# Where the last batch's output projection stands, and in which order units share a bank, in a transformer kernel on one core

## The chip, the cores and the metric

The kernel runs on one core of one Trainium2 chip. The metric is the device time of one execution in microseconds (us). The engines are called PE (TensorE), ACT (ScalarE), DVE (VectorE), POOL (GpSimd) and SP (SyncE, which here only issues DMAs).

## The reference

```python
x = x + attn(layernorm(x))     # 4 batches, 512 tokens, 256 wide, 16 heads of 16, with softmax
x = x + ffn(layernorm(x))      # silu(x W1^T) * (x W3^T), Walsh-Hadamard, W2^T; 1024 wide
x = x + mem(layernorm(x))      # gated decaying sum along the tokens
x = x + ffn(layernorm(x))
```

Inside `attn`: Q, K, V projections with bias, `scores = Q K^T / 4`, softmax over the keys, the weighted sum of V, and the output projection `out @ Wo.T + bo`. All is float32. The change touches the attention part alone.

## The kernel before

Each float32 product is made of three products of parts: a high part (rounded to the type fp32r) and a low part, what is left (`hi` on ACT, `lo` on POOL or DVE). "Splitting" a tile below means these two operations.

**Steps.** The attention of all four batches is one loop of 128 steps, `K = 32 b + s`: `b` is the batch and `s` (0 to 31) the step in it. A step serves two heads and one tile of 128 keys. In it PE makes two scores with the keys as rows (`score_kq`), ACT takes their exponentials (L921), and at each odd step PE weighs the values of the step pair before the last (`weigh_values`, four matmuls of 32 rows, each in two passes). So that the softmax can't overflow, the maximum of each row of the scores must be known before. For it PE makes each score a second time with the queries as rows, `LEAD = 13` steps ahead (`score_qk`), and DVE takes the maximum of each (`row_max`, L1096). So steps 0 to 18 of the last batch still have maxima beside them, and its steps 19 to 31 have none.

**Groups of maxima.** Eight steps make a group `S`. Once its maxima are there, POOL splits them (`split_max`, `ms<-mxr`, L1362 and L1364), PE turns them (`turn_maxima`, L590), ACT copies them out (`mT`) and SP copies two rows of them into `ring` (`max_copy`), from where the scores of group `S` read them. The turn stands at `s % 8 == MAX_AT` (3), so the last group's stands at step 19 of the last batch, and its rows are first read at step 24.

**Shared bank.** One PSUM bank, `MB`, serves everything else in turn (`shared_bank`): transposes of the normalised x of the next batch (`LN_AT`), its Q and K projections (`QK_AT`), its V projections (`V_AT`) and the output projection of the batch before (`OUT_AT`), of which each half has two parts, one per pair of groups. Each user waits until the one before has been read out; ACT reads out projections and turned maxima, DVE adds the output projection to X (`add_attention`, L1178). In batch 0 the W2 matrix is transformed in these places instead (`HAD_AT`). Each engine runs its own program in order, so a wait holds up everything behind it on that engine. The output projection at batch `b` is that of batch `b - 1`; the one of the last batch itself is made after the loop, in the first MLP chunk.

**Attention output.** Every two groups DVE has a transposed output `AOf`; ACT takes its high part (`AOh`), POOL its low part (`output_lo`, `AOl<-AOf,AOh`, L1342). The first of a batch is split at steps 28 (ACT) and 29 (POOL), the second at steps 5 and 6 of the next batch. `place_values` on POOL adds the bias to V. From step 19 of the last batch DVE and POOL also split the two MLP weights (`ring<-ring`, L1184, L1088, L1342), which the MLP waits for.

**Prologue.** Before step 0 the first batch's maxima of 13 steps are made. POOL there makes the first butterflies of the W2 transform (`fly`, X and PR), takes low parts of q and k (`first_lo`), splits the first maxima, places values; SP and ACT issue DMAs into `ring`.

Of the kernel before, what the change touches and what calls it, by code (L numbers as in the profile page):

```python
# [17 lines left out]
GROUPS = 4  # L18
# [10 lines left out]

LN_AT = (0, 2)  # L30
QK_AT = ((4, 6), (8, 10), (12, 14), (16, 18))
OUT_AT = ((20,), (24, 26))
V_AT = ((22,), (28, 30))

MAX_AT = 3
NORM_AT = (26, 19, 19)
STAT_AT = (18, 12, 12)

# [19 lines left out]
def build(nc, x, wq, wk, wv, wo, bqk_d, bv, bo, mv_, mg, mq, bgq_d, mo, w1, w2, w3, ident_d, had_d, out):  # L58
    ctx = ExitStack()
    with ctx:  # L60
# [197 lines left out]
        def max_copy(S, blk):  # L258
# [2 lines left out]
            r = HALF * blk + MROW  # L261
            return ring[r:r + 2, b % 2, QI, 2 * g:2 * g + 2, :].bitcast(F32), mT[16 * blk:16 * blk + 16, :]

        block = ctx.enter_context(nc.Block())


        @block.sync
        def _(sp):
# [58 lines left out]
                    sp.dma_start(*args).then_inc(ring_in[qk], DMA)  # L327

            ring_load(0, 2)
            ring_load(0, 3)  # L330

            for e in range(2):
# [5 lines left out]
            for b in range(BATCH):  # L338
                for s in range(STEPS):
                    if b == 0 and s == 0:  # L340
                        layout(W_UP, 0, 4, w1)
                        layout(W_LIN, 0, 4, w3)
                    if b == 0 and s == 9:

                        sp.wait_ge(fly_done, 5)
                        for c in range(2, BATCH):
                            sp.dma_start(X[:, c * TT:(c + 1) * TT, :], xv[c, :, :, :]).then_inc(x_in[c], DMA)
                    if b == BATCH - 1 and s == 0:

                        sp.wait_ge(st_ready, 2 * STEPS * b)  # L350
                        weights_in(W_UP)
                        weights_in(W_LIN)
                    if s % 8 == MAX_AT:
                        S = (STEPS * b + s + LEAD) // 8 - 1
                        if S < LAST_GROUP:
                            max_rows(S)
                    if b == 0 and s == 24:

                        for j, src in enumerate((mv_, mg, mq, mo)):
                            layout(W_MEM, j, 1, src)  # L360
                    if b < BATCH - 1:
                        for n in range(4):
                            if s == QK_AT[n][-1] + 2:
                                ring_load(b + 1, n)
# [25 lines left out]
        def _(pe):  # L390
# [189 lines left out]
            def turn_maxima(S, b, s):  # L580

                pe.wait_ge(ml_done, S + 1)
                pe.wait_ge(mt_ready, S)
                if s // 8 == 0:
                    pe.wait_ge(x_f, 2 * (b + 1))
                elif s // 8 < 3 and b < BATCH - 1:
                    pe.wait_ge(qk_f, 4 * b + 2 * (s // 8))
                elif s // 8 == 3:
                    pe.wait_ge(*((x_done, 2 * b) if b else (w2h_done, 3)))
                nc.tensor.transpose(MB[0:32, 0:P], ms[:, :, :, :].rearrange("p a b k -> p (a b k)"), ident[:, :])\  # L590
                    .then_inc(mps_ready, 1)

            def shared_bank(K, b, s):

                more, turned = b < BATCH - 1, (K + LEAD) // 8
                if b and s == LN_AT[0]:

                    pe.wait_ge(xns_ready, b + 1)
                    pe.wait_ge(*((v_copied, 2 * b + 2) if b > 1 else (w2h_done, 4)))
                    ln_transpose(0, MB)  # L600
                if s == LN_AT[b > 0]:
                    pe.wait_ge(x_f, 2 * b + 1)
                    ln_transpose(1, MB)
                for n in range(4):
                    if s in QK_AT[n] and more:
                        if s == QK_AT[n][0]:
                            if n % 2:
                                pe.wait_ge(qk_f, 4 * b + n)
                            else:
                                pe.wait_ge(mt_ready, turned)  # L610
                        i = 3 * QK_AT[n].index(s)
                        project_qk(b + 1, n, range(i, i + 3))
                if b == 0 and s in HAD_AT:

                    j = HAD_AT.index(s)
                    if j == 0:
                        pe.wait_ge(fly_done, 5)
                        pe.wait_ge(mt_ready, turned)
                    elif j == 2:
                        pe.wait_ge(w2h_done, 2)  # L620
                    else:
                        pe.wait_ge(v_copied, 3 + j // 3)
                    mm(MB, had[:, :], fly_half(j // 2)[:, j % 2 * SEQ:(j % 2 + 1) * SEQ], True, True)\
                        .then_inc(had_ready, 1)
                if s == OUT_AT[0][0] and b:
                    pe.wait_ge(aol_done, 2 * b)
                    pe.wait_ge(mt_ready, turned)
                    for part in range(2):
                        out_projection(0, part)
                if s in OUT_AT[1] and b:  # L630
                    if s == OUT_AT[1][0]:
                        pe.wait_ge(*((v_copied, 2 * b + 3) if more else (x_done, 2 * b - 1)))
                    out_projection(1, OUT_AT[1].index(s))
                if s == V_AT[0][0] and more:
                    pe.wait_ge(*((x_done, 2 * b - 1) if b else (w2h_done, 1)))
                    for part in range(2):
                        project_v(b + 1, 0, part)
                if b == 0 and s == V_FIRST_AT[1][0]:
                    pe.wait_ge(mt_ready, turned)
                    for part in range(2):  # L640
                        project_v(1, 1, part)
                if b and s in V_AT[1] and more:
                    if s == V_AT[1][0]:
                        pe.wait_ge(mt_ready, turned)
                    project_v(b + 1, 1, V_AT[1].index(s))

            for K in range(STEPS * BATCH):
                b, s = K // STEPS, K % STEPS
                for h in range(2):
                    wait_kq(K, h)  # L650
                    if K + LEAD < STEPS * BATCH:
                        wait_qk(K + LEAD, h)
                    score_kq(K, h)
                    if K + LEAD < STEPS * BATCH:
                        score_qk(K + LEAD, h)

                shared_bank(K, b, s)
                if K % 2 and K >= 3:
                    weigh_values((K - 3) // 2)
                S = (K + LEAD) // 8 - 1  # L660
                if s % 8 == MAX_AT and S < LAST_GROUP:
                    turn_maxima(S, b, s)

            def ffn_begin():
# [126 lines left out]
        def _(act):  # L791
# [111 lines left out]
            v_evacuate(0, 0, PS[:, V_BANK[0], :])  # L903
            max_evacuate(0, OB)
            act.wait_ge(mt_ready, 1)
            for blk in range(2):
                act.dma_start(*max_copy(0, blk)).then_inc(mrow_in, DMA)  # L907
            v_evacuate(0, 1, PS[:, V_BANK[1], :])
            ln_evacuate(1, 0, MB)
            ln_hi(1, 0, 0)  # L910
# [3 lines left out]
            for K in range(STEPS * BATCH):  # L914
# [29 lines left out]
                    ln_hi(b + 1, 0, 0)  # L944
                if s == LN_AT[b > 0] + 1:
                    ln_hi(b + 1, 1, 0)
                if K == 3:
                    act.wait_ge(wo_in, 8 * DMA)
                    hi(WOh[:, :, :].rearrange("p g n -> p (g n)"), OT[:, :, :].rearrange("p a c -> p (a c)"))\
                        .then_inc(whi_done, 1)  # L950
                if s == 5 and b:
                    act.wait_ge(aof_ready, 2 * b)
                    hi(AOh[:, 3, :], AOf[:, :]).then_inc(aoh_done, 1)
                if s == OUT_AT[1][-1] + 2:
                    act.wait_ge(aof_ready, 2 * b + 1)
                    if b:
                        act.wait_ge(wo_ready, 2 * b)
# [1 line left out]
                if b < BATCH - 1:  # L959
                    for n in range(4):  # L960
                        if s == QK_AT[n][-1] + 1:
                            qk_split(b + 1, n)
                if s % 8 == MAX_AT and (K + LEAD) // 8 - 1 < LAST_GROUP:
                    max_evacuate((K + LEAD) // 8 - 1)
            act.wait_ge(aof_ready, 2 * BATCH)
            hi(AOh[:, 3, :], AOf[:, :]).then_inc(aoh_done, 1)

# [77 lines left out]
        def _(dve):  # L1045
# [143 lines left out]
            for K in range(STEPS * BATCH):  # L1189
                b, s = K // STEPS, K % STEPS  # L1190
                for h in range(2):
                    if K + LEAD < STEPS * BATCH:
                        row_max(K + LEAD, h)
                    if b and h == 0:
                        for half in range(2):
                            if s == OUT_AT[half][-1] + 1:
                                add_attention(b - 1, half)
                S = K // 8 - 1
                if S >= 0:
# [132 lines left out]
        def _(pool):  # L1332
# [105 lines left out]
            for h in range(2):  # L1438

                v, w = (u.rearrange("p (m u n) -> p m u n", u=2, n=D) for u in (fly_raw(h), fly_near(h)))  # L1440
                fly(v[:, :, 0, :], v[:, :, 1, :], w[:, :, 0, :], w[:, :, 1, :])
            first_lo(2)
            first_lo(3)
            split_max(0)
            for h in range(2):

                pool.wait_ge(fly_done, h + 1)
                v, w = fly_near(h), fly_raw(h)
                fly(v[:, 0:SEQ], v[:, SEQ:], w[:, 0:SEQ], w[:, SEQ:])
            pool.wait_ge(const_in, 3 * DMA)  # L1450
            pool.wait_ge(vone_done, 1)
            place_values(0, 0)
            pool.wait_ge(zero_done, 1)
            x_lo_part(1, 0, 0)
            for g in range(1, GROUPS):
                place_values(0, g)

            for K in range(STEPS * BATCH):
                b, s = K // STEPS, K % STEPS
# [7 lines left out]
                    x_lo_part(b + 1, 1, 0)  # L1467
                if s == 6 and b:
                    output_lo(2 * b)
                if s == OUT_AT[1][-1] + 3:  # L1470
                    output_lo(2 * b + 1)
                if b and s in PLACE_MORE:
                    place_values(b, 1 + PLACE_MORE.index(s))
                if b < BATCH - 1:
# [2 lines left out]
                            qk_lo_part(b + 1, n)  # L1477
                    if s == PLACE_AT:
                        place_values(b + 1, 0)
                if K == 5:  # L1480
                    pool.wait_ge(whi_done, 4)
                    lo(WOl[:, :, :].rearrange("p g n -> p (g n)"), OT[:, :, :].rearrange("p a c -> p (a c)"),
                       WOh[:, :, :].rearrange("p g n -> p (g n)")).then_inc(wol_done, 1)
                if K == 4:

                    pool.wait_ge(lnT_ready, 4)
                    pool.wait_ge(x_hi, 4)
# [92 lines left out]
```

## Time and profile before

| | |
|---|---|
| median of 3 runs | 565.23 us |
| the three runs | 564.77, 565.23, 567.7 us |
| the profiled execution's own time | 566.53 us |
| its span | 564.7 us |
| mean granted PE clock | 0.997 |

The profile is of one execution. Its span runs from the first to the last instruction; 1.83 us of its time lie around the span. Times in the trace are us from the span's start. The duration of an instruction contains its latency, so instructions that follow each other closely overlap in it: the distance from start to start is what one costs.

### The profile page before, as it was taken

The numbers are of one execution on the slowest core, as the hardware profiler recorded it, in microseconds if no ns is written. First come the engines' busy times: TensorE is split into PE (matmuls) and PEld (weight loads), VectorE is DVE, ScalarE is ACT, GpSimd is POOL, SyncE is SP. The second block draws the span as 40 slices with busy tenths as digits, with TensorE's granted clock in tenths as the row PEclk, the third lists the DMA queues.
The fourth block names the chain that finished last, engine by engine and source line by source line (L and its number), as shares of the span: only waits on it lengthen the run. The fifth ranks groups of instructions, "written<-read, shape, count | busy, mean of one in ns | idle before, by whom it ended". The sixth has DMA issues, their size and how long they took to land.

```text
span 564.7 us, 8930 instructions
## 1 busy us (share of the span) xinstructions
PE 552.5 (98%) x3220; PEld 383.0 (68%) x3220; DVE 382.9 (68%) x729; ACT 311.8 (55%) x581; POOL 178.4 (32%) x209
## 2 busy tenths in 40 slices
PE   8999999999999998999999999999999999999997
PEld 4543343344434433468888888888888888988887
DVE  6988888898898899836465545746886437363333
ACT  3668889876987797743233223366775333323231
POOL 5794467562546242520202002233332010100100
PEclk9989999999999999999999999999999999999999
DMA  7354540231023030021001020110000210112101
GB/s 231 100 180 146 168 132 3 68 128 34 3 94 133 6 147 3 2 74 25 15 7 31 1 38 2 21 18 1 0 2 1 37 39 15 23 38 38 38 1 37
DMA packets 48443, 29.41 MB, mean 52 GB/s; under 512 B 33496, under 2 KB 41688, under 8 KB 48016
## 3 DMA queue, kind: packets, MB, share of 16 engines
q1 hardware_dynamic: 47180, 27.77, 17.1%
q10 hardware_dynamic: 1220, 1.07, 0.7%
q8 instruction: 26, 0.43, 0.3%
q14 instruction: 17, 0.14, 0.1%
HBM read 10.89 MB, written 5.24 MB: 29 GB/s over the span
## 4 chain that ended last, share of the span: by engine, by line
PE 91%; DVE 4%; ACT 2%; issue 1%; DMA 1%; ACTq 0%; POOL 0%; SPq 0%; POOLq 0%
PE PS L392 89%; DVE mxr L1096 2%; PE PS L403 1%; ACT PR L921 1%; PE PS L590 1%; DMA ring<-mT 1%; DMA X<-in_x 1%; DVE OT L1161 0%; ACTq L883 0%; DVE X L1265 0%; DVE X L1178 0%; ACTq L907 0%; DVE bst L1050 0%; PE PS L527 0%; POOL rstd L1338 0%
## 5 line engine op out<-in xcount | busy, mean ns | idle before, releaser
L392 PE MATMUL PS<-xTh,ring 128*128 128x512 f32 x608 | 188.1, 391 | 0.0
L1096 DVE TENSOR_REDUCE mxr<-PS 128x1 f32<-128x512 f32 x256 | 162.9, 680 | 25.5 <-PE PS L392 24.6
L921 ACT ACTIVATE PR<-PS 128x512 f32<-128x512 f32 x256 | 138.0, 602 | 30.3 <-PE PS L392 29.9
L392 PEld LDWEIGHTS PS<-xTh,ring 128*128 128x128 f32 x608 | 113.2, 188 | 23.7 <-issue 1.7
L392 PE MATMUL PS<-xTl,ring 128*128 128x512 f32 x304 | 110.1, 391 | 0.0
L793 ACT ACTIVATE AOh<-PR 128x512 fp32r<-128x512 f32 x72 | 45.5, 632 | 111.4 <-DVE PR L1235 105.9
L392 PE MATMUL PS<-ring 50*128 50x512 f32 (+1 forms) x512 | 100.0, 454 | 4.4 <-DVE mxr L1096 2.8
L1342 POOL TENSOR_TENSOR xTl<-xf,xTh 128x512 fp32r<-128x512 f32 x30 | 42.4, 1428 | 164.9 <-ACT xTh L793 164.9
L1235 DVE TENSOR_TENSOR PR<-PR,PS 128x512 f32<-128x512 f32 x64 | 43.4, 678 | 71.9 <-PE PS L392 51.8
L392 PEld LDWEIGHTS PS<-ring 50*128 50x128 f32 (+1 forms) x512 | 41.6, 185 | 71.1 <-ACT PR L921 43.2
L1088 DVE TENSOR_TENSOR AOl<-PR,AOh 128x512 fp32r<-128x512 f32 x72 | 51.0, 709 | 45.5 <-ACT AOh L793 45.4
L989 ACT ACTIVATE PR<-PS 128x512 f32<-128x512 f32 x64 | 37.9, 592 | 66.0 <-PE PS L392 65.9
L392 PE MATMUL PS<-W2h,AOh 128*128 128x256 f32 x256 | 72.4, 283 | 0.0
L392 PE MATMUL PS<-W2l,AOh 128*128 128x256 f32 x256 | 72.4, 283 | 0.0
L392 PE MATMUL PS<-W2h,AOl 128*128 128x256 f32 x256 | 72.3, 282 | 0.0
L392 PE MATMUL PS<-PR,Vp 128*32 128x512 f32 x512 | 69.1, 612 | 0.8 <-ACT PR L921 0.8
L392 PEld LDWEIGHTS PS<-xTl,ring 128*128 128x128 f32 x304 | 57.0, 188 | 10.1
L392 PEld LDWEIGHTS PS<-W2h,AOl 128*128 128x128 f32 x256 | 48.9, 191 | 2.1 <-DVE AOl L1088 0.2
L392 PEld LDWEIGHTS PS<-W2l,AOh 128*128 128x128 f32 x256 | 48.9, 191 | 1.9
L392 PEld LDWEIGHTS PS<-W2h,AOh 128*128 128x128 f32 x256 | 48.9, 191 | 0.0
L1335 POOL TENSOR_TENSOR veps<-mom,eps 128x4 f32<-128x4 f32 x16 | 3.2, 200 | 78.3 <-DVE mom L1056 78.3
L392 PEld LDWEIGHTS PS<-PR,Vp 128*32 128x32 f32 x512 | 10.1, 108 | 22.7 <-issue 18.4
(134 smaller groups left out, 623.6 us busy)
## 6 DMA issues: line engine op xcount, KB each, us to landing
ring<-qh SPq DMA_DIRECT2D x48, 128.0 KB, 2.8
xf<-PR SPq DMA_DIRECT2D x112, 32.0 KB, 1.9
ring<-ql SPq DMA_DIRECT2D x24, 128.0 KB, 2.8
ring<-weight_scratch SPq DMA_DIRECT2D x3, 1024.0 KB, 4.8
weight_scratch<-in_w SPq DMA_DIRECT2D x2, 1024.0 KB, 6.8
X<-in_x SPq DMA_DIRECT2D x3, 512.0 KB, 4.7
out<-X SPq DMA_DIRECT2D x6, 256.0 KB, 2.2
X<-in_w SPq DMA_DIRECT2D x1, 1024.0 KB, 5.5
```

Source lines behind the costliest of these rows:

```text
L392: return nc.tensor.matmul(dst, lhsT, rhs, start=start, stop=stop, skip_group_check=True)
L403: last = nc.tensor.transpose(bank[:, t * P:(t + 1) * P], XNs[:, t, dt * P:(dt + 1) * P], ident[:, :])
L590: nc.tensor.transpose(MB[0:32, 0:P], ms[:, :, :, :].rearrange("p a b k -> p (a b k)"), ident[:, :])\
L793: return nc.scalar.activation(dst, src, ACT.Copy, scale=scale)
L921: nc.scalar.activation(PR[:, j % 8, :], PS[:, kq_bank(j), :], ACT.Exp, scale=HD ** -0.5)\
L989: nc.scalar.activation(PR[:, f % 2, :], PS[:, f % 2, :], ACT.Silu).then_inc(sg_done, 1)
L1088: return nc.vector.tensor_tensor(dst, src, h.bitcast(F32), ALU.subtract)
L1096: nc.vector.tensor_reduce(mxr[:, S % 2, blk, TT * p + t:TT * p + t + 1], PS[:, QK0 + i % 3, :], AX.X, ALU.max, negate=True).then_inc(max_d ...
L1235: nc.vector.tensor_tensor(PR[:, 2 + f % 2, :], PR[:, f % 2, :], PS[:, 2 + f % 2, :], ALU.mult)\
L1335: nc.gpsimd.tensor_tensor(veps[:, n0:n0 + count], mom[:, n0:n0 + count, 1], eps[:, n0:n0 + count], ALU.add)\
L1342: return nc.gpsimd.tensor_tensor(dst, src, h.bitcast(F32), ALU.subtract)
```

## The change

The output projection of batch 2, which the last batch carries out at steps 20, 24 and 26, stands at steps 8, 10, 12 and 14 there, where the other batches have Q and K projections. The last turn of maxima stands at step 20 instead of 19, and the last batch's first output is split at steps 21 and 22. In batches 1 and 2 the second half of V (steps 28, 30) and the second half of the output projection (24, 26) change places; the first output of these and of batch 0 is split at step 31 on ACT and at step 2 of the next batch on POOL. In the prologue, POOL runs half of the second butterflies ahead of the split of the first maxima and of the last low part of k; the three later `place_values` go from ahead of the loop to step 4, the butterflies from step 4 to 5; ACT's and POOL's split of Wo go from steps 3 and 5 to 6 and 7; one of the first two row copies goes from ACT's queue to SP's.

```diff
-OUT_AT = ((20,), (24, 26))
-V_AT = ((22,), (28, 30))
-MAX_AT = 3
+OUT_AT = ((20,), (28, 30))
+V_AT = ((22,), (24, 26))
+LAST_OUT_AT = ((8, 10), (12, 14))
+MAX_AT, LAST_MAX_AT = 3, 20
+AO_AT, LAST_AO_AT = STEPS - 1, 21
...
+        def out_at(b):
+            return LAST_OUT_AT if b == BATCH - 1 else OUT_AT
+        def turned_at(K):
+            S = (K + LEAD) // 8 - 1
+            if S == LAST_GROUP - 1:
+                return S if K % STEPS == LAST_MAX_AT else None
+            return S if K % 8 == MAX_AT and S < LAST_GROUP else None
...
             ring_load(0, 2)
+            sp.wait_ge(mt_ready, 1)
+            sp.dma_start(*max_copy(0, 0)).then_inc(mrow_in, DMA)
             ring_load(0, 3)
...
                 if s // 8 == 0:
                     pe.wait_ge(x_f, 2 * (b + 1))
-                elif s // 8 < 3 and b < BATCH - 1:
+                elif b == BATCH - 1:
+                    pe.wait_ge(x_done, 2 * b - 2 + s // 8)
+                elif s // 8 < 3:
                     pe.wait_ge(qk_f, 4 * b + 2 * (s // 8))
-                elif s // 8 == 3:
-                    pe.wait_ge(*((x_done, 2 * b) if b else (w2h_done, 3)))
+                else:
+                    pe.wait_ge(*((v_copied, 2 * b + 4) if b else (w2h_done, 3)))
...
                     pe.wait_ge(xns_ready, b + 1)
-                    pe.wait_ge(*((v_copied, 2 * b + 2) if b > 1 else (w2h_done, 4)))
+                    pe.wait_ge(*((x_done, 2 * b - 2) if b > 1 else (w2h_done, 4)))
                     ln_transpose(0, MB)
...
-                if s == OUT_AT[0][0] and b:
-                    pe.wait_ge(aol_done, 2 * b)
-                    pe.wait_ge(mt_ready, turned)
-                    for part in range(2):
-                        out_projection(0, part)
-                if s in OUT_AT[1] and b:
-                    if s == OUT_AT[1][0]:
-                        pe.wait_ge(*((v_copied, 2 * b + 3) if more else (x_done, 2 * b - 1)))
-                    out_projection(1, OUT_AT[1].index(s))
+                for half in range(2):
+                    at = out_at(b)[half]
+                    if b and s in at:
+                        if s == at[0]:
+                            pe.wait_ge(aol_done, 2 * b)
+                            pe.wait_ge(mt_ready, turned)
+                        for part in range(2) if len(at) == 1 else (at.index(s),):
+                            out_projection(half, part)
...
                     if s == V_AT[1][0]:
-                        pe.wait_ge(mt_ready, turned)
+                        pe.wait_ge(v_copied, 2 * b + 3)
                     project_v(b + 1, 1, V_AT[1].index(s))
...
-            for blk in range(2):
-                act.dma_start(*max_copy(0, blk)).then_inc(mrow_in, DMA)
+            act.dma_start(*max_copy(0, 1)).then_inc(mrow_in, DMA)
...
-                if K == 3:
+                if K == 6:
                     act.wait_ge(wo_in, 8 * DMA)
...
-                if s == OUT_AT[1][-1] + 2:
+                if s == (LAST_AO_AT if b == BATCH - 1 else AO_AT):
                     act.wait_ge(aof_ready, 2 * b + 1)
...
-                            if s == OUT_AT[half][-1] + 1:
+                            if s == out_at(b)[half][-1] + 1:
                                 add_attention(b - 1, half)
...
+            def fly_next(h):
...
-            first_lo(2)
-            first_lo(3)
-            split_max(0)
-            for h in range(2):
...
+            first_lo(2)
+            fly_next(0)
+            split_max(0)
+            first_lo(3)
+            fly_next(1)
...
             x_lo_part(1, 0, 0)
-            for g in range(1, GROUPS):
-                place_values(0, g)
...
-                if s == OUT_AT[1][-1] + 3:
+                if s == 2 and b:
+                    output_lo(2 * b - 1)
+                if s == LAST_AO_AT + 1 and b == BATCH - 1:
                     output_lo(2 * b + 1)
...
-                if K == 5:
+                if K == 7:
                     pool.wait_ge(whi_done, 4)
...
                 if K == 4:
+                    for g in range(1, GROUPS):
+                        place_values(0, g)
+                if K == 5:
```

The loops of SP, PE and ACT ask `turned_at(K)` for the group to turn, where they compared `s % 8` with `MAX_AT` before.

## Rows read from the trace of the kernel before

**Rows 1.** The page's busy times: us, share of the span, instructions.

```profile
PE 552.5 (98%) x3220; PEld 383.0 (68%) x3220; DVE 382.9 (68%) x729; ACT 311.8 (55%) x581; POOL 178.4 (32%) x209
```

**Rows 2.** PE's waits: who waited for whom, us in total, times, longest.

```profile
PE PS L590 <- DVE X L1178: 0.5, 2, 0.3
```

**Rows 3.** PE by stretches: window, us, busy, granted clock, DMA share, GB/s.

```profile
39.20:42.61 3.41, 3.41 (x16) 0.50 0.89 347
...
210.00:222.00 12.00, 10.10 (x69) 1.00 0.01 4
```

**Rows 4.** Timeline of ACT, batch 2: start, us, operation, count, idle before.

```profile
156.72 1.09 ACT L921 ACTIVATE PR<-PS 128x512 f32<-128x512 f32 x2
...
159.94 1.09 ACT L921 ACTIVATE PR<-PS 128x512 f32<-128x512 f32 x2 [0.57 <-PE PS L392]
...
163.38 1.09 ACT L921 ACTIVATE PR<-PS 128x512 f32<-128x512 f32 x2
...
169.84 1.09 ACT L921 ACTIVATE PR<-PS 128x512 f32<-128x512 f32 x2
...
187.66 1.08 ACT L921 ACTIVATE PR<-PS 128x512 f32<-128x512 f32 x2 [0.58 <-PE PS L392]
...
191.43 1.09 ACT L921 ACTIVATE PR<-PS 128x512 f32<-128x512 f32 x2 [0.16 <-PE PS L392]
```

**Rows 5.** Timeline of ACT, batch 3, steps 8 to 31.

```profile
209.88 2.07 ACT L921 ACTIVATE PR<-PS 128x512 f32<-128x512 f32 x4 [0.88 <-PE PS L392]
...
221.60 2.07 ACT L921 ACTIVATE PR<-PS 128x512 f32<-128x512 f32 x4 [0.77 <-PE PS L392]
224.43 2.06 ACT L921 ACTIVATE PR<-PS 128x512 f32<-128x512 f32 x4 [0.77 <-PE PS L392]
...
239.19 0.63 ACT L793 ACTIVATE AOh<-AOf 128x512 fp32r<-128x512 f32 x1
239.71 3.04 ACT L921 ACTIVATE PR<-PS 128x512 f32<-128x512 f32 x6
```

**Rows 6.** Timeline of PE, batch 3, steps 3 to 31.

```profile
203.31 0.28 PE L590 MATMUL PS<-ident,ms 128*32 128x128 f32 x1
...
219.64 0.50 PE L392 MATMUL PS<-ring 50*128 50x512 f32 x2 [0.43 <-DVE mxr L1096]
...
226.77 0.28 PE L590 MATMUL PS<-ident,ms 128*32 128x128 f32 x1 [0.81 <-POOL ms L1364]
...
232.18 0.49 PE L392 MATMUL PS<-ring 50*128 50x512 f32 x2
...
233.51 0.49 PE L392 MATMUL PS<-ring 50*128 50x512 f32 x2
233.94 1.07 PE L392 MATMUL PS<-PR,Vp 128*32 128x512 f32 x8
...
240.85 1.06 PE L392 MATMUL PS<-PR,Vp 128*32 128x512 f32 x8 [0.77 <-ACT PR L921]
```

**Rows 7.** Timeline of POOL, batch 3, steps 1 to 6.

```profile
201.06 1.28 POOL L1342 TENSOR_TENSOR xTl<-xf,xTh 128x512 fp32r<-128x512 f32 x1 [3.14 <-ACT xTh L793]
...
202.67 0.22 POOL L1364 TENSOR_TENSOR ms<-mxr,ms 128x16 fp32r<-128x16 f32 x1
...
206.74 1.28 POOL L1342 TENSOR_TENSOR AOl<-AOf,AOh 128x512 fp32r<-128x512 f32 x1
```

**Rows 8.** Timeline of ACT where batch 0 goes over into batch 1.

```profile
89.23 2.21 ACT L921 ACTIVATE PR<-PS 128x512 f32<-128x512 f32 x4
```

**Rows 9.** Timeline of PE, steps 0 and 3 of batch 0.

```profile
34.58 0.95 PE L392 MATMUL PS<-ring 50*128 50x512 f32 x4 [0.25 <-DMA ring<-mT]
...
39.21 1.93 PE L392 MATMUL PS<-PR,Vp 128*32 128x512 f32 x8
```

**Rows 10.** Timeline of DVE: before step 4 of batch 0, and batch 3 from step 19.

```profile
30.48 9.87 DVE L1096 TENSOR_REDUCE mxr<-PS 128x1 f32<-128x512 f32 x16 [0.16 <-PE PS L392]
...
227.33 0.71 DVE L1172 STREAM_TRANSPOSE AOf<-OTn 128x512 f32<-128x512 f32 x1 [0.96 <-POOL OTn L1381]
...
232.26 1.65 DVE L1088 TENSOR_TENSOR ring<-ring 128x512 fp32r<-128x512 f32 x1
...
237.30 0.99 DVE L1088 TENSOR_TENSOR ring<-ring 128x512 fp32r<-128x512 f32 x1
```

More of the change, by code:

```diff
@@ L352, in _ @@
                         weights_in(W_LIN)
[L353 to L356, printed above, removed]
+                    S = turned_at(STEPS * b + s)
+                    if S is not None:
+                        max_rows(S)
                     if b == 0 and s == 24:
@@ L659, in _ @@
                     weigh_values((K - 3) // 2)
-                S = (K + LEAD) // 8 - 1
-                if s % 8 == MAX_AT and S < LAST_GROUP:
+                S = turned_at(K)
+                if S is not None:
                     turn_maxima(S, b, s)
@@ L962, in _ @@
                             qk_split(b + 1, n)
-                if s % 8 == MAX_AT and (K + LEAD) // 8 - 1 < LAST_GROUP:
-                    max_evacuate((K + LEAD) // 8 - 1)
+                S = turned_at(K)
+                if S is not None:
+                    max_evacuate(S)
             act.wait_ge(aof_ready, 2 * BATCH)
```

## The prediction, before the change was run

> **What bounds the kernel now.** I read the page's busy times first, then the list of waits, then the timelines of ScalarE (ACT), TensorE and GpSimd (POOL) stage by stage. The page is to be read for one thing: TensorE (PE) is busy 98% of the span [rows 1]; its recorded waits are small [rows 2]. So time moves only where PE's own work is moved into a hole, or where PE is made to wait. The edits touch only the attention part, up to about 243 us; behind it PE is busy without such waits, so I count what the attention part gains or loses as the result.
>
> The timeline of ACT gives the length of each step: its two exponentials are issued once a step, so the start of a row is the start of a step. Steps 8 to 15 of batch 2, with the next batch's projections beside the maxima, last from 156.72 to 169.84, 13.12 us [rows 4]. The same steps of batch 3, which have nothing beside the maxima, last from 209.88 to 221.60, 11.72 us [rows 5], and in them PE waits 0.43 us a pair of steps for VectorE's maxima [rows 6]. That is a hole. From step 19 of batch 3 there are no more maxima; there the output projection stands in line with the last scores, and ACT's last exponential ends at 239.71 + 3.04 = 242.75 [rows 5].
>
> **Part 1, the last batch's output projection moved to steps 8 to 14.** One part of it costs PE 232.18 to 233.51 less the score pair in front, which is 233.51 to 233.94: 1.33 - 0.43 = 0.90 us [rows 6]. It is about what three projection matmuls cost a pair of steps in batch 2, so steps 8 to 15 should come to the 13.12 us of [rows 4] with one difference. The half of X that VectorE adds at step 11 must be read out of the shared bank before PE turns the maxima at that same step. That constellation exists before, at steps 26 and 27 of batches 1 and 2: 187.66 to 191.43, 3.77 us, against 159.94 to 163.38, 3.44 us, where the turn waits for no add [rows 4]; the list of waits has PE's two waits for X [rows 2]. So 13.12 + 0.33 = 13.45, and 0.90 instead of 0.89 changes nothing: **+1.75 us**. Low bound 1.4 (no collision at step 11), high bound 4 x 0.90 = 3.6 if the hole took none of it; I take the near end, since batch 2 shows the same work fitted in.
>
> **Part 2, what the tail gives back.** Without the projection the tail is bound by ACT, so I lay out its work. Steps 18 to 31 have 28 exponentials, and six in a row take 3.04, so one costs 0.48 and the last one ends 0.16 after its slot [rows 5]. From 224.43: 28 x 0.48 = 13.44, the split of the attention output 0.52 (239.19 to 239.71) [rows 5], the copy of the turned maxima about 0.25, the tail of the last one 0.16: 238.80. PE can keep up: a pair of steps beside the maxima is four score pairs and a weighing of values, 2.83 us (221.60 to 224.43) [rows 5] less the hole of 0.43; with 1.06 for the weighing [rows 6] a score pair is 0.34, so a pair of steps in the tail, two score pairs and a weighing, is 1.74 us, against 1.92 for four exponentials. What ACT splits at step 21 is VectorE's transpose, done at 227.33 + 0.71 = 228.04 [rows 10]; ACT comes there at about 228.5. The last turn of maxima now comes behind the scores of step 20, so PE's 0.81 us wait for POOL [rows 6] shrinks to about 0.5, and it is no longer on the path that sets the end. The gain is 242.75 - 238.80 = **-4.0 us**. Bounds: -3.4, PE's projection time alone, to -5.0, with PE's waits of 0.81 and 0.77 [rows 6] gone as well.
>
> What is queued behind: the two rows of maxima that SP's queue copies for step 24 are issued some 0.3 us later than before (mT 227.6, not 227.4) but are wanted 1.2 us sooner, at 231.0. VectorE's split of the MLP's weights ended at 237.30 + 0.99 = 238.29 [rows 10]; with two adds fewer and one POOL split (1.28 us) more among them it ends between 237 and 239, and the MLP wants it at 239.9. Both hidden, with about 0.6 and 1 us to spare.
>
> The Trainium skill, "SBUF — State Buffer", section on SBUF's two separate sides, says that VectorE and GpSimd share a port pair that is locked for a whole instruction when VectorE has two SBUF inputs. The trace agrees in kind: a split of these weights took 1.65 us at 232.26 and 0.99 at 237.30 [rows 10]. By that rule the added POOL split can cost the chain all of its 1.28 us; 239.0, still short of 239.9, so the sum stays the same by either.
>
> **Part 3, value and output units change places (batches 1 and 2).** At steps 26 and 27 there is no add before the turn any more, so those pairs go from 3.77 to 3.44 us [rows 4]: **-0.66 us** for two batches. The add moves to step 31, where no turn follows in the same step; the transposes of the next step 0 stand behind two score pairs and a weighing, some 1.6 us later. Bounds: 0, if the wait shows up there instead, to -0.66.
>
> **Part 4, the POOL split that goes from step 29 to step 2.** This is the part that costs. POOL at steps 1 to 3 of a batch: it splits the transposed x, 201.06 to 202.34, then at once makes the high and the low part of the maxima, which end at 202.67 + 0.22 = 202.89. PE turns them at 203.31 [rows 6, 7]. The new split stands between those two in POOL's order, since the one in front waits for ACT's xTh and starts no sooner. It takes 1.28 (the same split at 206.74) [rows 7], so the maxima are ready at 204.17 and PE, which came at 203.31, stands 0.86 us. Behind PE's turn stand the next scores, and for those wait both ACT and VectorE; in batches 1 and 2 PE has no hole later to make it up, in batch 3 VectorE sets the pace and loses the same. In batch 1 there is more: ACT's split of the output moves to step 31, where ACT goes without idle time from step 31 into step 0 (four exponentials in 2.21 against 2.07 elsewhere, a slack of 0.14) [rows 5, 8]; 0.52 - 0.14 = 0.38 us later comes xTh, and with it all of POOL's chain. Batch 1: 1.24, batches 2 and 3: 0.86 each, **+2.96 us**. In batches 2 and 3 ACT has the place, since the value copy left step 30. Bounds: 0, if POOL does the split in its idle time before, to 3 x 1.28 + 0.38 = 4.2.
>
> **Part 5, the prologue.** VectorE's sixteen maxima from 30.48 on run without a gap to 40.35 [rows 10], so they set the pace, and the reordered POOL work (first half of the butterflies, then the maxima's split, then the last split of k) leaves the maxima's split where it was, since it waits for the maxima. One of the two row copies goes by SP's queue instead of ACT's: PE's wait of 0.25 us at 34.58 for them goes [rows 9], **-0.2 us**. The load of the last k rows follows the copy on SP's queue and is issued about 1.4 us later; it is wanted only at step 3. Three placings of values move from ahead of POOL's second split of x to step 4; that split waits for ACT anyway, so the turn at step 3 gains next to nothing. ACT's split of Wo goes from step 3 to step 6 where ACT is nearly full: 0 to 0.5, I take **+0.15**.
>
> The clock stretch deserves its own sentence: at 39.20 to 42.61 the granted clock was 0.50 (the 1.2 GHz level) [rows 3], after steps in which PE had scores alone, with waits between them. The weighing that began at 39.21 took 1.93 [rows 9] instead of 1.06 [rows 6]. I leave this stretch where it is, because the change moves hardly any PE work into the steps before it.
>
> **Sum**: +1.75 - 4.0 - 0.66 + 2.96 - 0.2 + 0.15 = 0.0 us. Made against the profiled execution's own 566.53 us it stays 566.5. That execution is 1.30 above the median of the runs, 565.23, so I predict **565.3 us**.
>
> **Rivals.** *(A) POOL's moved split is hidden.* For it: POOL is idle 3.14 us before 201.06. Against: the order of its program puts the split behind the one that this idle time waits for. Sum without +2.96: 562.3 us; chance 0.14. *(B) The slow clock stretch goes.* The turn and the scores at step 3 and 4 then run at the full level: 1.93 - 1.06 for the weighing and some 0.6 for turn and four scores, -1.5 us, 563.8. For it: PE's work shifts by 0.2 us; against: it shifts nothing else there. Chance 0.18. The Trainium skill, "TensorE: Matmul & The Clock Gate", section on what you observe and what happens, says that the point where the clock changes varies from run to run, which would let (B) come without any cause in the change; the spread of the three runs, 564.77 to 567.7, neither shows nor excludes it. *(C) Slower: the tail falls to the slow clock.* Without the projections PE is busy 1.74 of 1.92 us a pair of steps. If the clock drops there for 3.41 us as at 39.20, PE does 1.7 us of work where 3.1 are due: +1.4, 566.7. It decides where PE's idle share is much above that of the maxima stage of batch 3, whose holes (0.43 of 2.83) left the clock at 1.00 [rows 3]. Chance 0.08. *(D) The maxima's rows for step 24 land late*, over 231.0 less 0.5: each us more is a us lost; if they take 3.0 us from the issue of the second copy at 228.3, +0.8, 566.1. Chance 0.10.
>
> **How the numbers follow.** Forecast 0.42, (A) 0.14, (B) 0.18, (C) 0.08, (D) 0.10, none of these 0.08. About 0.5%, 2.8 us, is what a measurement of this kernel tells from no change: under 562.4 is faster, over 568.1 slower. (A) falls on that edge, and with (B) beyond it; none of the rivals alone reaches 568.1. Faster 0.16, same 0.77, slower 0.07. The range 562.2 to 567.4 just holds (A), and the prices of (B), (C) and (D) and the bounds of part 5; it leaves out the unnamed cases and (A) with more besides.
>
> **What would show it.** Steps 8 to 15 of batch 3 at about 13.45 us; from the last step with maxima to the last exponential 14.4 instead of 18.3; PE waiting for POOL's low part of the maxima near step 3 of batches 1 to 3, about 1.2, 0.9 and 0.9 us; step pairs 26 and 27 at 3.44. I am wrong if there is no such wait, if the tail stays at 18, or if the granted clock differs from before in a stretch.

## The result, and the profile after

The changed kernel takes 570.95 us (median of 5 runs, 569.79 to 581.22) beside 565.23 us (median of 5 runs, 564.77 to 567.7): the ratio is 1.0093, with a 95% interval of 1.0072 to 1.0113. It is slower by 0.9%, clear of the 0.5% that I had named, and outside the range I gave (562.2 to 567.4).

The first profile of it was taken in an execution of 581.22 us, in which the granted clock was at its lower level for two long stretches, 20.5 us from 38.7 and 10.2 us from 246.9. A second profile of the same kernel (own time 569.88 us, span 568.1, mean granted clock 0.996) is nearer to the median, and the rows below are of that one. The page's busy times:

```profile
PE 553.6 (97%) x3220; PEld 383.1 (67%) x3220; DVE 385.9 (68%) x729; ACT 311.9 (55%) x581; POOL 178.4 (31%) x209
```

PE has lost one per cent of its busy share. Its waits (waited for, us in total, times, longest us):

```profile
PE PS L407 <- DVE OT L1177: 3.7, 1, 3.7
PE PS L607 <- POOL ms L1380: 2.6, 4, 1.0
```

The first wait did not exist before: one wait of 3.7 us for VectorE's transpose into `OT`. The second is the one I had forecast, POOL's low part of the maxima, at step 3 of batches 1 to 3; its fourth time, at step 20 of batch 3, stands for the single 0.8 us at step 19 before.

The timeline of ACT, with the starts of steps 26 and 28 of batch 2, and of steps 8 and 16 of batch 3 and its end:

```profile
188.38 1.09 ACT L936 ACTIVATE PR<-PS 128x512 f32<-128x512 f32 x2 [0.58 <-PE PS L407]
...
191.84 1.09 ACT L936 ACTIVATE PR<-PS 128x512 f32<-128x512 f32 x2 [0.16 <-PE PS L407]
...
211.04 1.09 ACT L936 ACTIVATE PR<-PS 128x512 f32<-128x512 f32 x2 [0.86 <-PE PS L407]
...
224.43 2.11 ACT L936 ACTIVATE PR<-PS 128x512 f32<-128x512 f32 x4 [0.57 <-PE PS L407]
227.40 3.08 ACT L936 ACTIVATE PR<-PS 128x512 f32<-128x512 f32 x6 [0.86 <-PE PS L407]
...
231.47 0.62 ACT L809 ACTIVATE AOh<-AOf 128x512 fp32r<-128x512 f32 x1
232.00 5.97 ACT L936 ACTIVATE PR<-PS 128x512 f32<-128x512 f32 x12
242.08 4.27 ACT L936 ACTIVATE PR<-PS 128x512 f32<-128x512 f32 x8 [4.12 <-PE PS L407]
```

Against [rows 4]: the pair of steps 26 and 27 takes 3.46 us instead of 3.77. Against [rows 5]: steps 8 to 15 take 13.39 instead of 11.72, and step 18 to the last exponential 242.08 + 4.27 - 227.40 = 18.95 instead of 18.33. The tail goes at ACT's full pace for twelve exponentials, as I had laid it out, and then ACT stands idle for 4.12 us. PE in the same stretch:

```profile
235.09 0.73 PE L407 MATMUL PS<-ring 50*128 50x512 f32 x4
239.54 1.78 PE L407 MATMUL PS<-PR,Vp 128*32 128x512 f32 x8 [3.72 <-DVE OT L1177]
241.25 1.22 PE L407 MATMUL PS<-ring 50*128 50x512 f32 x4
242.40 1.42 PE L407 MATMUL PS<-PR,Vp 128*32 128x512 f32 x8
```

The weighing at 239.54 is the first of the last group. It writes the bank that VectorE's transpose of the group before must have read (`pe.wait_ge(ot_done, S)` in `weigh_values`). VectorE meanwhile:

```profile
230.93 4.02 DVE L1200 CAST ring<-ring 128x512 fp32r<-128x512 f32 x4
234.99 1.65 DVE L1104 TENSOR_TENSOR ring<-ring 128x512 fp32r<-128x512 f32 x1
236.56 1.48 DVE L1200 CAST ring<-ring 128x512 fp32r<-128x512 f32 x1
238.08 0.69 DVE L1104 TENSOR_TENSOR ring<-ring 128x512 fp32r<-128x512 f32 x1
238.69 0.71 DVE L1177 STREAM_TRANSPOSE OT<-PS 128x512 f32<-128x512 f32 x1
```

It works through the MLP's weights without idle time and comes to the transpose at 238.69. PE had finished what the transpose reads at about 235.1. So the transpose was held up by what stands ahead of it in VectorE's program. In the kernel before the same two instructions, the transpose and PE's weighing behind it, were:

```profile
235.07 0.72 DVE L1161 STREAM_TRANSPOSE OT<-PS 128x512 f32<-128x512 f32 x1
...
236.69 1.06 PE L392 MATMUL PS<-PR,Vp 128*32 128x512 f32 x8
```

There the transpose ended at 235.79, 0.9 us before PE came. Counted from the start of step 18 (224.43 before, 227.40 now), PE comes 3.8 us sooner than before, and the transpose ends 0.6 us later.

Behind the wait the granted clock is at 0.50 (PE: window, us, busy, clock, DMA share, GB/s), and the last weighings cost 1.4 to 1.8 us instead of 1.06:

```profile
210.00:224.40 14.40, 14.12 (x101) 1.00 0.01 3
...
239.80:243.20 3.40, 3.40 (x16) 0.50 0.02 5
```

POOL at the head of batch 3 answers to [rows 7]:

```profile
201.46 1.28 POOL L1358 TENSOR_TENSOR xTl<-xf,xTh 128x512 fp32r<-128x512 f32 x1 [9.05 <-ACT xTh L809]
202.69 1.28 POOL L1358 TENSOR_TENSOR AOl<-AOf,AOh 128x512 fp32r<-128x512 f32 x1
203.91 0.20 POOL L1378 CAST ms<-mxr 128x16 fp32r<-128x16 f32 x1
204.19 0.22 POOL L1380 TENSOR_TENSOR ms<-mxr,ms 128x16 fp32r<-128x16 f32 x1
```

and PE turns the maxima only then:

```profile
202.74 1.06 PE L407 MATMUL PS<-PR,Vp 128*32 128x512 f32 x8
204.47 0.28 PE L607 MATMUL PS<-ident,ms 128*32 128x128 f32 x1 [0.66 <-POOL ms L1380]
```

### The profile page after: what moved, and what is told of

Its sections match the earlier page's. It is cut to its first block, busy times and chain, and to the rows that moved or that the text cites. A ratio compares the mean times of both kernels' runs of the same rounds, so it can differ in the third digit from the quotient of the medians.

```text
span 579.4 us, 8933 instructions
## 1 busy us (share of the span) xinstructions
PE 563.5 (97%) x3220; PEld 385.7 (67%) x3220; DVE 385.1 (66%) x729; ACT 312.4 (54%) x581; POOL 177.7 (31%) x209
## 3 DMA queue, kind: packets, MB, share of 16 engines
q10 hardware_dynamic: 1202, 1.06, 0.6%
## 4 chain that ended last, share of the span: by engine, by line
PE 80%; DVE 7%; issue 6%; POOL 5%; DMA 1%; ACT 1%; ACTq 0%; SPq 0%; POOLq 0%
PE PS L407 79%; DVE mxr L1112 3%; DVE ring L1200 1%; POOL XNs L1361 1%; POOL Vp L1387 1%; PE PS L418 1%; DVE OT L1177 1%; DMA X<-in_x 1%; POOL xTl L1358 1%; POOL AOl L1358 1%; POOL W2l L1358 0%; PE PS L607 0%; DVE bst L1066 0%; POOL OTn L1397 0%; POOL rstd L1354 0%
## 5 line engine op out<-in xcount | busy, mean ns | idle before, releaser
L407 PE MATMUL PS<-ring 48*128 48x512 f32 (+1 forms) x512 | 104.0, 471 | 2.2 <-DVE mxr L1112 0.8
L407 PEld LDWEIGHTS PS<-ring 48*128 48x128 f32 (+1 forms) x512 | 42.8, 193 | 73.5 <-ACT PR L936 38.5
L407 PE MATMUL PS<-PR,Vp 128*32 128x512 f32 x512 | 73.9, 651 | 3.9 <-DVE OT L1177 3.7
L407 PEld LDWEIGHTS PS<-xTl,ring 128*128 128x128 f32 x304 | 57.1, 188 | 10.2
```

The costliest lines, as they stand in the source:

```text
L407: return nc.tensor.matmul(dst, lhsT, rhs, start=start, stop=stop, skip_group_check=True)
```

## The experiments

Theory V: the loss is the wait for VectorE's transpose, which stands behind splits of the MLP's weights. Rival C: the granted clock falls in the tail or the prologue by itself, and the wait is a small part. Beside them stand POOL's moved split and the prologue as smaller terms. Except for the two single runs, ratios are to the kernel before, run beside the others on the same chip; its medians in the three sets of runs were 565.39 us (the first four experiments), 566.2 (the next four) and 565.67 (the last two).

**The change again.** No edit.

> The changed kernel itself, for a second profile, since in the first one the granted clock was at its lower level for 20.5 us from 38.7 and for 10.2 us from 246.9. Theory V (VectorE's order in the tail): PE still waits 3.5 to 3.9 us for VectorE's transpose of the output near step 27 of batch 3, because that transpose stands behind six splits of MLP weights; the clock stretch behind it is a consequence and may be shorter. Theory C (the clock is the cause by itself): with a shorter stretch at the lower level the wait shrinks too, to under 2 us. Both: steps 3 of batches 1 to 3 at about 2.5 us, as in the first profile.

Measured: one run of 569.88 us; the wait is 3.72 us as in the first profile (3.74), and steps 3 take 2.60, 2.49 and 2.50 us. The lower clock lasted 3.4 us in the tail here and 10.2 there, and the wait did not change with it: against C. Here it began at 239.8, when the wait was over.

**VectorE's splits of the second weight behind the transpose.**

```diff
+SPLIT_STEPS = (19, 20, 21, 22, 26, 27, 28, 29)
-                if b == BATCH - 1 and SPLIT_AT <= s < SPLIT_AT + 8:
-                    w_split_hi((s - SPLIT_AT) // 4, (s - SPLIT_AT) % 4)
+                if b == BATCH - 1 and s in SPLIT_STEPS:
+                    i = SPLIT_STEPS.index(s)
+                    w_split_hi(i // 4, i % 4)
```

> The changed kernel with one edit: VectorE splits the second MLP weight at steps 26 to 29 of batch 3, behind the transpose of step 25, and not at 23 to 26. Theory V: the 3.7 us wait goes, the stretch from step 18 to the last exponential falls from about 19 to 20 us to 14.4 to 15, and the time falls by 4 to 6 us, to 565 to 567. Theory C: the clock falls there anyway, the time stays at 570 to 571. Rival L (the MLP then waits for the late splits): the wait moves behind the last step, 1 to 2 us, time 566 to 569.

Measured: 566.46 us, ratio to the kernel before 1.0022 (0.9996 to 1.0048): 4.5 us less than the changed kernel. The wait of 3.7 us is gone, and the tail runs through at ACT's pace. ACT:

```profile
235.47 3.08 ACT L937 ACTIVATE PR<-PS 128x512 f32<-128x512 f32 x6 [0.86 <-PE PS L408]
238.44 0.26 ACT L810 ACTIVATE mT<-PS 32x128 f32<-32x128 f32 x1
238.60 1.06 ACT L937 ACTIVATE PR<-PS 128x512 f32<-128x512 f32 x2
239.55 0.62 ACT L810 ACTIVATE AOh<-AOf 128x512 fp32r<-128x512 f32 x1
240.07 9.88 ACT L937 ACTIVATE PR<-PS 128x512 f32<-128x512 f32 x20
```

From 235.47 to 249.95 are 14.48 us; my sum had 14.37. In the whole tail the clock stayed at its full level in this profile. The MLP did not wait for the later splits (rival L falls): from the last exponential to the end of the span are 321.8 us, 321.7 in the changed kernel.

**POOL's split at step 0.**

```diff
-                if s == 2 and b:
+                if s == 0 and b:
                     output_lo(2 * b - 1)
```

> The changed kernel with one edit: POOL makes the low part of the last output at step 0 of the next batch, ahead of its idle time, and not at step 2. If the 0.7 to 0.8 us by which step 3 of batches 1 to 3 grew come from this split in front of the maxima's, steps 3 go back from 2.5 to about 1.8 us and the time falls by 2.2 us, to 568.7. If they come from the later split on ACT (step 31) alone, nothing falls: 570.9.

Measured: 570.82 us, ratio 1.0084 (1.0053 to 1.0115). The median hardly moved, but the trace shows the term: steps 3 of batches 1 to 3 take 1.63, 1.76 and 1.76 us instead of 2.60, 2.49 and 2.50, in all 2.44 less. The wait of 3.7 us is still there, and in five of the seven runs the mean granted clock was 0.988 or less, in only one of the five runs of the changed kernel. In runs with the same mean clock, 0.994, this kernel took 568.15 and 568.59 us and the changed one 570.71, 570.95 and 571.63: 2.6 us apart in the middle, near the 2.44 of the trace. Why so many of its runs had a lower clock stays open.

**Both.** The two edits above together.

> The changed kernel with both edits of the two kernels before. Theory V with the POOL term: the gains add, 4 to 6 and 2.2 us, time 562.5 to 565, under the kernel before. Theory C: 568.7.

Measured: 563.87 us, ratio 0.9955 (0.9928 to 0.9982), below the kernel before. The longest wait of PE in the tail is 0.3 us.

**The last batch's edits alone.** The kernel before with the edits that concern batch 3: `out_at`, `turned_at`, and

```diff
-                if s == OUT_AT[1][-1] + 2:
+                if s == (LAST_AO_AT if b == BATCH - 1 else OUT_AT[1][-1] + 2):
...
-                if s == OUT_AT[1][-1] + 3:
+                if s == (LAST_AO_AT + 1 if b == BATCH - 1 else OUT_AT[1][-1] + 3):
                     output_lo(2 * b + 1)
```

> The kernel before with the last batch's edits alone: its output projection at steps 8 to 14, the last turn of maxima at step 20, the last output split at steps 21 and 22. Theory V: all of the tail's loss is in this part. Steps 8 to 15 take 13.5 us instead of 11.7, PE waits 3.5 to 3.9 us for VectorE's transpose, and the tail (step 18 to the last exponential) takes 18 to 20 us instead of 18.3: in all +1.8 to +3.5 us, 567.2 to 569 beside 565.4. If the tail needs the other edits to go wrong, it takes 14.4 us and the time is 563.2.

Measured: 571.43 us, ratio 1.0079 (1.0053 to 1.0104). Its waits:

```profile
PE PS L403 <- DVE OT L1176: 3.7, 1, 3.7
```

Steps 8 to 15 take 13.49 us and the tail 18.92. So the loss of the tail needs nothing else of the change. The median lies above what I expected; its two runs of mean clock 0.994 took 568.19 and 568.74 us, in the expected span, and the rest had lower clocks. In its profile the lower clock also stood for 17.1 us from 22.9 and for 6.8 us from 46.8, far ahead of the wait, and that part of the time is not explained by the tail.

**The last batch's edits with the late splits.** The kernel of before with these edits and `SPLIT_STEPS`.

> The kernel before with the last batch's edits and VectorE's splits of the second MLP weight behind the transpose of step 25. Theory V: tail 14.4 to 14.5 us, steps 8 to 15 13.5, time -2.1 us against the kernel before, 563.3. It has neither the swap of steps 24 to 30 (-0.65) nor the two extra splits; the two kernels should lie under 0.5 us apart.

Measured: 562.88 us, ratio 0.9947 (0.9924 to 0.997). Steps 8 to 15 take 13.49 us, the tail 14.49. So the idea of the change was worth about 2 us in the kernel before, once the one thing behind which it waited was out of the way: the trace gives 1.77 + 0.12 - 3.84 = -1.95 us (steps 8 to 15, steps 16 and 17, the tail), and among runs with a mean clock of 0.999 or 1.000 the medians are 562.85 and 565.04, 2.2 apart. The ratio shows more, 3.0 us, because 16 of the 24 runs of the kernel before had a lower clock and only 2 of these 10.

**Both, with the prologue as before.** The changed kernel with the two edits of "Both", called mends from here on, and all prologue edits taken back (POOL's order, the row copy on ACT's queue, placings, ACT's split of Wo at step 3 and POOL's at step 5).

> The kernel with both mends (weight splits late, POOL's split at step 0) and with all prologue edits taken back. If the prologue edits cost (ACT's split of Wo at step 6: steps 4 to 31 of batch 0 took 48.6 to 48.75 us instead of 48.13), those steps fall back to 48.1 and the time falls by 0.3 to 0.5 us, to 563.4. If they gain as I took it, it rises by 0.2.

Measured: 563.1 us, ratio 0.9931 (0.9894 to 0.9968). Steps 4 to 31 of batch 0 take 48.27 us instead of 48.63: the prologue edits cost 0.4 us there. One profile of each carries this; the two times, 563.1 and 563.87, point the same way and do not settle it.

**The last output split late.** The change with `LAST_AO_AT = 28`.

> The changed kernel, but with the last batch's first output split at steps 28 (ACT) and 29 (POOL), not 21 and 22. It tells apart the order on VectorE and the port that VectorE shares with GpSimd. If the order of the program decides, PE still waits at least 2.4 us for the transpose, by no more than 1.3 us less than 3.7. If the added POOL split holds VectorE up, the wait falls under 2 us.

Measured: one run of 570.92 us. The wait is 2.73 us. VectorE:

```profile
231.69 4.04 DVE L1200 CAST ring<-ring 128x512 fp32r<-128x512 f32 x4
235.76 1.65 DVE L1104 TENSOR_TENSOR ring<-ring 128x512 fp32r<-128x512 f32 x1
237.33 0.41 DVE L1200 CAST ring<-ring 128x512 fp32r<-128x512 f32 x1
237.78 0.69 DVE L1104 TENSOR_TENSOR ring<-ring 128x512 fp32r<-128x512 f32 x1
238.39 0.71 DVE L1177 STREAM_TRANSPOSE OT<-PS 128x512 f32<-128x512 f32 x1
```

POOL beside it, in the changed kernel and here:

```profile
236.05 1.71 POOL L1358 TENSOR_TENSOR ring<-ring 128x512 fp32r<-128x512 f32 x1
...
232.62 4.24 POOL L1358 TENSOR_TENSOR ring<-ring 128x512 fp32r<-128x512 f32 x3 [0.36 <-DVE ring L1200]
```

POOL's last split of the weights ended at 237.76 in the changed kernel, while VectorE's cast at 236.56 was under way; here it ended at 236.86, before VectorE's cast at 237.33. With POOL's extra split out of the way that cast takes 0.41 instead of 1.48 us, and the wait falls by 1.0 of 3.7. The tail stayed as long, 18.86 us, since the clock was low for 6.8 us there. The other 2.7 us remain with the order as it was. They are not the order alone: at 0.41 us a cast and 0.69 a low part, as they take beside an idle POOL, the five casts and two low parts from 230.93 on would be done in some 3.4 us, at 234.4 (an estimate from these rows), before PE had made what the transpose reads. They took 7.8. So the wait needs both, the splits ahead of the transpose and their slow pace beside POOL's own splits. Moving the splits removes it; that a faster pace would too is not tested.

**The kernel before with the late splits.**

> The kernel before with one edit: VectorE splits the second MLP weight at steps 26 to 29. Theory V says that the splits stood in nobody's way before the change, since there the transpose was done at 235.8 and PE wanted it at 236.7: tail 18.3 us, the time as before within 0.3 us. If the late splits are worth something by themselves (a general gain that has nothing to do with the change), the time falls by 1 us or more.

Measured: 566.33 us, ratio 0.9997 (0.9966 to 1.0027), tail 18.32. The splits stood in nobody's way there, so the gain of the mended kernels is no general one.

**The best version.** Both mends, the old prologue, and

```diff
-                if s == (LAST_AO_AT if b == BATCH - 1 else AO_AT):
+                if s == (28, AO_AT, AO_AT, LAST_AO_AT)[b]:
```

> The kernel with both mends and the old prologue, and batch 0's first output split on ACT at step 28 as before. Against the same kernel with that split at step 31 steps 4 to 31 of batch 0 fall from 48.3 to 47.9 us and the time by 0.3 to 0.4 us, to 562.7, about 2.5 us under the kernel before. If it gains nothing, ACT was not full at step 31.

Measured: 562.41 us, ratio 0.9945 (0.992 to 0.997), 3.3 us under the median of the kernel before beside it. Its profile has the lower clock level for 6.8 us from 39.8 on, in steps 3 to 5 of batch 0, so steps 4 to 31 as a whole can't be compared. But step 31 of batch 0 alone, from the start of its exponentials to that of the next step's, takes 1.13 us, as in the kernel before (1.12), against 1.47 in the kernel with the split at 31: the edit gives 0.34 us, as expected. It beats both kernels; whether it beats the one with the last batch's edits and the late splits alone (0.9947) is open.

## Why the prediction was wrong

**The step that failed** is Part 2, and in it the sentences on what is queued behind. I wrote that VectorE's split of the MLP's weights ends between 237 and 239, that the MLP wants it at 239.9, and called it hidden. That holds for the MLP. But in VectorE's program the transpose of step 25 stands behind the splits of steps 19 to 24 (six casts and two low parts), and PE's weighing of step 27 waits for it; I followed the splits to the engine that reads them and not to the instruction queued behind them on the same engine. They did end where I said (241.89, which is 238.92 if the later start of the tail is taken off). Before the change the transpose ended at 235.79 and PE came to its weighing at 236.69, so there were 0.9 us of slack and no row of waits. I took some 3.4 us of work from PE ahead of that point, so that it came 3.8 us sooner, and added a POOL split that holds VectorE up by 1.0 us. The sentence that PE can keep up with ACT left out that PE itself waits for VectorE. What was to be -4.0 us came out as +0.6 (18.95 against 18.33 us), and as +1.6 in the first profile, where the clock stayed low longer. "If the tail stays at 18" was my own sign of being wrong. Moving the splits brought the tail to 14.48 us: the sum of ACT's work was right.

**Part 1** was right: 13.39 and 13.49 us in the profiles, 13.45 forecast. Behind it steps 16 and 17 take 0.13 us longer than before, which I had not counted.

**Part 3** was right in kind and size: 3.46 us for the pair, -0.31 and -0.32.

**Part 4** was right in mechanism and a little too big: steps 3 grew by 0.83, 0.72 and 0.73 us, 2.28 in all, and moving the split to step 0 gave back 2.44. The 0.38 us that I had laid on POOL's chain in batch 1 came elsewhere: step 31 of batch 0, with ACT's split in it, takes 1.47 us instead of 1.12. With these 0.35 the part is 2.63, where I had 2.96.

**Part 5**: PE's wait of 0.25 us for the rows ahead of step 0 did not go. It is 0.19 in the changed kernel, where VectorE's maximum ends it:

```profile
34.93 1.01 PE L407 MATMUL PS<-ring 50*128 50x512 f32 x4 [0.19 <-DVE mxr L1112]
```

With the old prologue it is 0.20, for the rows. So the copy on SP's queue gained next to nothing, not 0.2: the maximum came as late as the rows. Steps 0 to 3 took 5.87 us with the clock at its full level in the changed kernel and 5.88 to 5.89 with the old prologue. Steps 4 to 31 of batch 0 took 48.56 us instead of 48.13; but the 48.13 begin at 42.23, inside the stretch of low clock, and the kernel with the last batch's edits and the late splits, which has the old prologue and no such stretch, took 47.92. Of the 0.64 between 48.56 and that, 0.35 belong to Part 4 as said, and 0.29 are left for the prologue edits (0.36 by the pair of kernels above); I had -0.2 + 0.15.

**The parts together.** At the full clock outside the tail, from step 4 of batch 0 on, they are in the second profile: Part 1 +1.80 (with the 0.13 of steps 16 and 17), Part 2 +0.62, Part 3 -0.63, Part 4 +2.63, Part 5 +0.29: +4.7 us. The whole stretch from step 4 of batch 0 to the last exponential took 204.99 us instead of 200.53, or of 200.32 without the low clock, also 4.7. The run of 569.88 us lies 4.9 above 564.98, the median of the thirteen runs of the kernel before beside it that had a mean clock of 0.999 or 1.000; the median run of the changed kernel, 570.95 us, takes 1.1 more, at a mean clock of 0.994 instead of 0.996. Of the miss of 4.7, 4.6 are Part 2; the errors of Parts 4 (-0.3) and 5 (+0.3) cancel, by luck.

**The rivals.** (A) is out: the split does hold the maxima up. (B) happened in the second profile: the stretch at 39.2 is gone there, steps 0 to 3 of batch 0 take 5.87 us instead of 7.08, and with the 0.2 of the steps behind (Part 5) that is 1.4, where I had 1.5. But no cause in the change is shown, since such stretches come and go between executions: the first profile of the same kernel has one of 20.5 us from 38.7. Of the twelve profiles six have one or two of 3.4 to 20.5 us between 22 and 60 us, and six none. Of the 24 runs of the kernel before beside the first four experiments, thirteen had a mean granted clock of 0.999 or 1.000 and took 564.75 to 565.5 us, seven had 0.997 and took 566.21 to 566.97; their medians, 564.98 and 566.69, are 1.7 us apart, near the 1.5 that I read from [rows 3] and [rows 9], though no trace of these runs shows where their low clock stood. (C) happened, but as a consequence and not by itself: in the tails without the wait (seven profiles, that of before among them) the clock never fell, and in all five profiles with the wait it did, 2.1 to 4.6 us after PE had come to a stop. (D) is out: in the tail no profile has a wait of PE for the rows of over 0.15 us. The slower outcome came by a path that I had not named.

## What to carry to other kernels

When work is taken from the engine that sets the pace, ask what each other engine's program has in front of every instruction that this engine waits for, and by how much it was early: a release that is 0.9 us early shows no wait, and the wait appears once the reader comes sooner. "Hidden" must hold for everything queued behind the hidden work on its engine, not only for the one who reads its output. And read the gain stage by stage: here the other stages did nearly what was forecast, and nearly all of the miss stood in one row of the list of waits.

## What the runs showed of the hardware

VectorE and GpSimd held each other up more than I had expected when both work on SBUF (the on-chip memory that holds these tiles): four casts took 4.02 us in the tail, against 0.38 to 0.42 for one that runs beside no POOL work, a POOL split took up to 1.71 instead of 1.28, and one more POOL split cost VectorE 1.0 us. The Trainium skill, "SBUF — State Buffer", section on SBUF's two separate sides, says that VectorE, with two SBUF inputs or in one of its two-port modes, and GpSimd take a shared pair of ports, and that the one that starts first has it for its whole instruction. The cast of 1.48 instead of 0.41 us agrees with that, as it ended at 238.04, just behind POOL's split (237.76); whether a cast runs in a two-port mode no run here shows.

The granted clock fell to 0.50 in every profile in which PE stood for 2.7 to 3.7 us in the tail, for 3.4 to 10.2 us, though PE was busy before and behind. A wait of 3.7 us so cost the tail 4.4 to 5.5 us (18.92 to 19.94 against 14.48), and one of 2.7 us cost 4.4 (18.86). Why it stayed low for 3.4 us in one execution and for 10.2 in another stays open.
